# Sums of routed rows in a macaron mixture-of-experts kernel: the first choice weighed and added in one VectorE operation a tile, the second weighed on ScalarE

## The chip, the cores and the metric

One core of one Trainium2 chip runs the kernel. The time is device microseconds of one execution; three executions of the kernel before gave 1242.54, 1244.09 and 1245.39 us, so the median is 1244.09 us. The engines are TensorE (PE, its weight loads PEld), VectorE (DVE), ScalarE (ACT), GpSimd (POOL) and SyncE (SP, which issues most DMAs).

## The reference

The input is x of 8 batches of 1024 tokens of 256 channels, in float32. Three steps follow each other, all residual:

- x = x + 0.5 * FFN(layernorm(x))
- x = x + attention(layernorm(x)), a linear attention with relu on queries and keys, 16 heads
- x = x + 0.5 * FFN(layernorm(x)), the same weights

FFN is a mixture of 16 experts plus a shared expert. For each token a softmax gate chooses two experts (out of the two best of four groups), and the routed part is

```
y = w1 * expert_a(x) + w2 * expert_b(x)
```

with w1 and w2 the gate's scores of the first and the second choice. The change touches only this weighted sum and its adding to x.

## The kernel before, in words

All of x stays in SBUF as `xres`, 8 batches of 8 tiles; a tile is 128 tokens by 256 channels. An FFN first routes (scores, choices, ranks; rows of normalised tokens are scattered to DRAM in the order of experts), then runs 143 tiles of expert rows, whose outputs are scattered to a DRAM tensor `routed_rows` in the order (choice, token). The shared expert's work is cut into parts ("up" is two matmul groups with a silu on ScalarE and a gating on VectorE, "down" is a matmul group with two adds on VectorE), and these parts are spread over the stages: 19 of them are held back for the end of the second FFN (lines 248 and 257).

Both choices' rows come back from DRAM by DMA into a buffer `y` with the choice as an index of its own, and are weighed and added to `xres`. The weights, one for each token (a column of 128 x 1) and choice, already hold the factor 0.5. This happens at two places.

**After the first FFN, two tiles at a time** (a pair; 4 pairs a batch, 32 in all). SP loads a pair into one of three buffers once the pair three back is added (line 476). ScalarE's `weigh_routed` (line 1025) waits for the load and multiplies each of the four tiles (two tokens' tiles, two choices) by its weight in place. VectorE's `combine` (line 1474) waits for that, adds first choice, then second choice to x as two operations of 128 x 512, and takes the layer norm's statistics. The first batch's four pairs come ahead of the attention. The pairs of batch b+1 are placed inside the attention loop of batch b: on ScalarE behind every second relu of the keys (line 1107), on VectorE around `sum_keys` (lines 1593 to 1613). TensorE waits for `sum_keys` at line 764 and for the keys' relu at lines 732 and 743. In the batches b = 1, 3 and 5 of that loop the normalising and first routing of a batch of the second FFN is also done (line 898 on ScalarE); in b = 2, 4 and 6 the rest of its choice (VectorE). I call them the odd and the even batches.

**After the second FFN, four tiles at a time** (a piece; 2 a batch, 16 in all). SP loads six pieces ahead, and each later one when the piece six before it is added (lines 498 to 505), then stores the finished piece to the output. ScalarE runs, in order, the silu of one held part and then `weigh_final` of a piece (lines 1143 to 1146), eight multiplications. VectorE runs, in order, the held part's gating (line 1364) or two adds (line 1374), then the piece's two adds of 128 x 1024 (lines 1660 and 1662). Five held parts lie ahead of the first piece, one ahead of each of the next twelve pieces (up or down; two ups to a down), none ahead of the piece numbered 13, and a last down part ahead of piece 14. TensorE computes the held parts meanwhile.

The order on every engine is the order of the program; semaphores alone join them. The two places of waiting are, on VectorE,

```
dve.wait_ge(s.weighted, n + 1)          # pair: ScalarE has weighed both choices
dve.wait_ge(s.f_weighted, n + 1)        # piece
```

Of the kernel before, what the change touches and what calls it, by code (L numbers as in the profile page):

```python
# [18 lines left out]
ALU, ACT, AX = mybir.AluOpType, mybir.ActivationFunctionType, mybir.AxisListType  # L19

P = 128
BATCHES, SEQ, C = 8, 1024, 256
TOKENS = BATCHES * SEQ
NT = SEQ // P
# [25 lines left out]
YSLOTS = 3  # L50
# [4 lines left out]
PIECES = 2  # L55
FSLOTS = 6
# [198 lines left out]
def held_ahead(n):  # L255

    return HELD[1][n + 4 if n else 0:n + 5]
# [55 lines left out]
def program(nc, m, d, sem):  # L313
    s = Names()
# [64 lines left out]
    def x_tiles(b, i, n):  # L379
        return m.xres[:, b, i:i + n, :].rearrange("p i c -> p (i c)")  # L380

    def piece(n):
        b, h = divmod(n, PIECES)
        return x_tiles(b, h * NT // PIECES, NT // PIECES)
# [19 lines left out]
    with nc.Block() as block:  # L404
        @block.sync
        def _(sp):
# [5 lines left out]
            def pads(L):  # L412
                sp.wait_ge(s.pads_ready, L + 1)
                _, starts = nc.values_load_multi_w_load_instructions(
                    m.pad_to[0:1, :], engines=(sp.engine,), min_val=0, max_val=SPARE - P,
                    skip_runtime_bounds_check_because="a region holds a row for every token and a tile more")
                for start in starts:
                    sp.dma_start(d.xg[bass.ds(start, P), :], m.pad[:]).then_inc(s.padded, 16)
# [468 lines left out]
        def _(act):  # L887
# [128 lines left out]
                                             bias=m.tile_b13[:, 0, i:i + 1]).then_inc(s.rsilu_ready, 1)  # L1016

            def weigh(b, tiles, y):
                for k in range(2):
                    for j, i in enumerate(tiles):  # L1020
                        last = nc.scalar.activation(y[:, k, j * C:(j + 1) * C], y[:, k, j * C:(j + 1) * C], ACT.Copy,  # L1021
                                                    scale=m.weights[:, b, k, i:i + 1])
                return last

            def weigh_routed(b, h):
                n = PAIRS * b + h
                act.wait_ge(s.routed_in[n % YSLOTS], 16 * (n // YSLOTS + 1))
                weigh(b, range(2 * h, 2 * h + 2), m.ylq[:, n % YSLOTS]).then_inc(s.weighted, 1)

            def weigh_final(n):  # L1030
                b, h = divmod(n, PIECES)
                act.wait_ge(s.f_loaded[n % FSLOTS], 16 * (n // FSLOTS + 1))
                weigh(b, range(h * NT // PIECES, (h + 1) * NT // PIECES), m.yf[n % FSLOTS]).then_inc(s.f_weighted, 1)
# [44 lines left out]
            for i in range(PAIRS):  # L1078
                last = nc.scalar.activation(m.xs[0][:, i, 0:C], m.xres[:, 0, i, :], ACT.Identity,
                                            bias=m.nmr[:, i:i + 1], scale=m.rstd[:, i:i + 1])  # L1080
# [68 lines left out]
        def _(dve):  # L1149
            TT, TR = nc.vector.tensor_tensor, nc.vector.tensor_reduce  # L1150
            ch = Chain(dve, s.dve_steps)
# [7 lines left out]
            def stats(b, tiles, own=m.own):  # L1159
                for i in tiles:  # L1160
                    last = nc.vector.bn_stats(own.stat[:, i, :], m.xres[:, b, i, :])  # L1161
                ch.did(last)
# [213 lines left out]
            def shared(L, n, work, steps):  # L1376
                b, kind, k = part_of(n)
                r = L * BATCHES + b
                if b == BATCHES or kind == "up":
                    for _ in range(steps):  # L1380
                        next(work, None)
                    if b < BATCHES:
                        gated(r, k)
                    return
                for j in range(2):
                    add_shared(r, 2 * k + j)
                    for _ in range(steps * j // 2, steps * (j + 1) // 2):
                        next(work, None)
# [61 lines left out]
            def experts(L):  # L1450
                for i in range(-1, TILES + 2):
# [11 lines left out]
                    if routed(i - 2):  # L1463
# [7 lines left out]
                            dve.wait_ge(s.rows_out[last_user % SLOTS], 16 * (last_user // SLOTS) + 16)  # L1471
                        TT(m.ry[(i - 2) % RYSLOTS], ry_ps[y % RB][:, 0:C], m.be2[:, bass.ds(e, C)], ALU.add).then_inc(s.ry_scaled, 1)  # L1472

            def combine(b, h):
                n = PAIRS * b + h
                y = m.ylq[:, n % YSLOTS]
                dve.wait_ge(s.bias_added, BIASED.index(b) + 1)
                x = x_tiles(b, 2 * h, 2)
                dve.wait_ge(s.weighted, n + 1)
                ch.then(TT(x, x, y[:, 0, :], ALU.add))  # L1480
                TT(x, x, y[:, 1, :], ALU.add).then_inc(s.combined, 1)
                dve.wait_ge(s.combined, n + 1)
                stats(b, range(2 * h, 2 * h + 2))
# [169 lines left out]
            for n in range(BATCHES * PIECES):  # L1653
                b, h = divmod(n, PIECES)
                x, y = piece(n), m.yf[n % FSLOTS]
                for part in held_ahead(n):
                    shared(1, part, iter(()), 0)
                dve.wait_ge(s.bias_added, BATCHES + BIASED.index(b) + 1)
                dve.wait_ge(s.f_weighted, n + 1)
                TT(x, x, y[:, 0, :], ALU.add).then_inc(s.f_added, 1)  # L1660
                dve.wait_ge(s.f_added, 2 * n + 1)
                TT(x, x, y[:, 1, :], ALU.add).then_inc(s.f_added, 1)

# [224 lines left out]
```

## Time and profile before

| what | us |
|---|---|
| median of three runs | 1244.09 |
| the profiled execution, its own time | 1243.24 |
| its span, first to last instruction | 1241.5 |
| PE busy | 1148.4 (93%) |
| DVE busy | 852.7 (69%) |
| ACT busy | 759.6 (61%) |
| POOL busy | 698.1 (56%) |

The 1.7 us between the span and the execution's own time lie around the instructions. Shares of busy time are means over stages that have different limits. The two places of the change lie at 457 to 750 us (the pairs) and at 1180 to 1238 us (the pieces).

How to read the rows: a line of a timeline has the start in us, the duration in us (of all instructions merged into the line), the engine, the line of the kernel, the operation, output and inputs, and in brackets the idle time before it and what ended that. Consecutive instructions of one engine may overlap a little, so merged durations are less than the sum of single ones.

### The profile page before, as it was taken

What the parts mean: (1) busy time and instruction counts of PE and PEld (TensorE: products, weight loads), DVE (VectorE), ACT (ScalarE), POOL (GpSimd) and SP (SyncE); (2) the same over time, 40 slices, a digit from 0 to 9 for tenths busy, and PEclk for the clock granted to TensorE, in tenths of its full rate; (3) what the DMA queues carried; (4) which work ended last, traced back from release to release, by engine and by line L of the source; (5) the groups of instructions that cost most, each with busy time, mean ns of one, the idle gap of its engine ahead of it and who ended that gap; (6) DMA issues with size and microseconds to landing.
All of it is one profiled execution on the core that took longest, in us unless ns stands there. A gap on an engine that the chain in (4) does not pass through costs nothing.

```text
span 1241.5 us, 26349 instructions
## 1 busy us (share of the span) xinstructions
PE 1148.4 (93%) x6696; PEld 904.6 (73%) x6696; DVE 852.7 (69%) x2774; ACT 759.6 (61%) x1698; POOL 698.1 (56%) x850
## 2 busy tenths in 40 slices
PE   7988999999999967899998999889998999999995
PEld 5555555899999946777887878545557999999653
DVE  6788784566666655768878786677844666666488
ACT  4454441688888845675655653544415888888398
POOL 3577776488888854000411503356763888887810
PEclk9999999999999998999999999899999999999997
DMA  9922227556555523012320400114585555555398
GB/s 360 309 91 95 98 104 201 172 172 174 171 172 156 164 104 105 32 38 68 112 72 24 133 22 35 35 69 141 171 210 180 173 170 174 173 157 162 119 400 333
DMA packets 94215, 181.53 MB, mean 146 GB/s; under 512 B 17624, under 2 KB 60400, under 8 KB 92022
## 3 DMA queue, kind: packets, MB, share of 16 engines
q1 hardware_dynamic: 66630, 110.44, 29.2%
q0 software_dynamic: 26016, 67.55, 15.3%
q10 hardware_dynamic: 1424, 1.86, 0.5%
q8 instruction: 59, 0.97, 0.3%
q14 instruction: 86, 0.70, 0.2%
HBM read 97.63 MB, written 86.08 MB: 148 GB/s over the span
## 4 chain that ended last, share of the span: by engine, by line
PE 58%; DVE 17%; ACT 11%; issue 5%; POOL 5%; DMA 3%; SPq 1%; DVEq 0%; ACTq 0%; POOLq 0%
PE bank L700 20%; PE bank L710 10%; PE bank L559 7%; PE bank L691 5%; POOL expert_rows L1683 4%; PE bank L575 4%; PE bank L806 3%; ACT rows L1021 3%; ACT w L1021 3%; DVE stat L1161 2%; PE bank L756 2%; PE bank L732 2%; ACT xn L1039 1%; PE bank L521 1%; ACT rows L898 1%
## 5 line engine op out<-in xcount | busy, mean ns | idle before, releaser
L700 PE MATMUL bank<-rows,att 128*128 128x128 f32 x2288 | 303.2, 276 | 0.3 <-ACT att L1010 0.3
L700 PEld LDWEIGHTS bank<-rows,att 128*128 128x128 f32 x2288 | 279.2, 192 | 0.8 <-ACT att L1010 0.6
L1683 POOL DMA_INDIRECT expert_rows<-rows,slots x160 | 155.4, 971 | 80.0 <-issue 57.3
L1010 ACT COPY att<-w 128x512 f32 x286 | 177.0, 619 | 10.2 <-issue 4.2
L1740 POOL DMA_INDIRECT routed_rows<-silu,rdest x160 | 158.3, 989 | 35.0 <-issue 24.6
L1458 DVE SCALAR_TENSOR_TENSOR rows<-bank,tile_b,att 128x128 f32<-128x128 f32 x286 | 100.1, 350 | 112.9 <-ACT att L1015 102.0
L710 PE MATMUL bank<-w,rows 128*128 x572 | 171.5, 382 | 4.3 <-DVE rows L1458 4.2
L1740 POOL DMA_INDIRECT routed_rows<-rows,rdest x126 | 124.7, 990 | 68.4 <-DVE rdest L1441 40.7
L1009 ACT COPY rows<-bank 128x256 f32<-128x256 f32 x286 | 106.6, 373 | 89.1 <-PE bank L691 86.9
L575 PE MATMUL bank<-ws,be 128*128 128x256 f32 x512 | 124.0, 388 | 8.6 <-DVE be L1364 8.6
L925 ACT ACTIVATE silu<-bank,bs 128x512 f32<-128x512 f32 x64 | 43.9, 686 | 127.6 <-PE bank L559 117.5
L575 PEld LDWEIGHTS bank<-ws,be 128*128 128x128 f32 x512 | 95.8, 194 | 35.4 <-DVE be L1364 18.5
L1729 POOL TENSOR_TENSOR xres<-xres,half_bs 128x128 f32<-128x128 f32 x256 | 118.0, 470 | 3.1
L691 PE MATMUL bank<-ident,rows 128*128 128x128 f32 x572 | 109.4, 274 | 3.4 <-DMA rows<-expert_rows 2.0
L1015 ACT ACTIVATE att<-bank,tile_b 128x128 f32<-128x128 f32 x286 | 103.8, 363 | 4.5 <-PE bank L700 4.5
L691 PEld LDWEIGHTS bank<-ident,rows 128*128 128x128 f32 x572 | 80.4, 142 | 32.7 <-issue 3.8
L710 PEld LDWEIGHTS bank<-w,rows 128*128 128x128 f32 x572 | 87.2, 192 | 5.6 <-issue 5.5
L1683 POOL DMA_INDIRECT expert_rows<-w,slots x48 | 48.3, 1006 | 59.9 <-PE bank L732 28.0
L1364 DVE SCALAR_TENSOR_TENSOR be<-bank,bs,silu 128x512 f32<-128x512 f32 x64 | 47.7, 749 | 48.3 <-PE bank L559 43.6
L1680 POOL TENSOR_TENSOR rstd<-ve,minus_half 128x8 f32<-128x8 f32 x8 | 15.0, 1880 | 113.4 <-DVE ve L1169 113.4
L1472 DVE TENSOR_TENSOR silu<-bank,be 128x256 f32<-128x256 f32 x160 | 67.9, 424 | 15.2 <-issue 6.3
L1021 ACT ACTIVATE rows<-rows,weights 128x256 f32<-128x256 f32 x176 | 73.8, 504 | 7.3 <-DMA rows<-routed_rows 7.3
(212 smaller groups left out, 2156.9 us busy)
## 6 DMA issues: line engine op xcount, KB each, us to landing
rows<-expert_rows SPq DMA_DIRECT2D x286, 129.5 KB
rows<-routed_rows SPq DMA_DIRECT2D x32, 512.0 KB, 4.2
w<-routed_rows SPq DMA_DIRECT2D x10, 1024.0 KB, 10.9
out<-xres SPq DMA_DIRECT2D x16, 512.0 KB, 9.3
xres<-in_x SPq DMA_DIRECT2D x7, 1024.0 KB, 9.5
rows<-routed_rows SPq DMA_DIRECT2D x6, 1024.0 KB, 7.7
expert_rows<-pad SPq DMA_DIRECT2D x47, 129.5 KB, 14.0
w<-in_w SPq DMA_DIRECT2D x1, 4096.0 KB, 24.4
```

Of the source, the lines that this page charges most:

```text
L575: last = nc.tensor.matmul(y_ps[j][:, t % 2 * C:(t % 2 + 1) * C], m.gT[:, g, mi, t * P:(t + 1) * P], m.ws2[:, mi, :], start=mi == 0, stop=m ...
L691: last = nc.tensor.transpose(rT_ps[a % 2][:, c * P:(c + 1) * P], m.rin[:, a % SLOTS, c * P:(c + 1) * P], m.ident[:])
L700: last = nc.tensor.matmul(rh_ps[t % RB][:, n * P:(n + 1) * P], m.rw13[:, t % RB, c * C + n * INTER:c * C + (n + 1) * INTER], m.rT[:, t % R ...
L710: nc.tensor.matmul(ry_ps[y % RB][:, 0:C], m.rgT[:, y % RB, :], m.w2[:, bass.ds(e, C)], start=True, stop=True).then_inc(s.ry_ready, 1)
L1009: nc.scalar.copy(m.rT[:, a % RB, :], rT_ps[a % 2][:, 0:C]).then_inc(s.rT_copied, 1)
L1010: nc.scalar.copy(m.rw13[:, a % RB, :].rearrange("p (c n) -> p c n", c=KC), w13[:, :, bass.ds(expert_at(i + 2), C)]).then_inc(s.rw13_copied, 1)
L1015: nc.scalar.activation(m.rsilu[:, t % RB, :], rh_ps[t % RB][:, 0:P], ACT.Silu, bias=m.tile_b13[:, 0, i:i + 1]).then_inc(s.rsilu_ready, 1)
L1021: last = nc.scalar.activation(y[:, k, j * C:(j + 1) * C], y[:, k, j * C:(j + 1) * C], ACT.Copy, scale=m.weights[:, b, k, i:i + 1])
L1458: nc.vector.scalar_tensor_tensor(m.rgT[:, t % RB, :], rh_ps[t % RB][:, P:2 * P], m.tile_b13[:, 1, i:i + 1], m.rsilu[:, t % RB, :], ALU.add ...
L1683: nc.gpsimd.indirect_dma_start(out=d.xg, out_offset=bass.IndirectOffsetOnAxis(ap=m.slots[:, slots_of(r), k, i:i + 1], axis=0), in_=m.xs[bu ...
L1729: last = nc.gpsimd.tensor_tensor(x, x, m.half_bs2[:, c:c + P], ALU.add)
L1740: nc.gpsimd.indirect_dma_start(out=d.yt, out_offset=bass.IndirectOffsetOnAxis(ap=m.rdest[:, n:n + 1], axis=0), in_=m.ry[i % RYSLOTS], in_o ...
```

## The change

ScalarE weighs only the second choice. VectorE weighs and adds the first choice's rows with one `scalar_tensor_tensor` a tile: x = y * weight + x, the weight being a column of 128 x 1. These operations wait for the load and not for ScalarE; the second choice's add waits for ScalarE as before, and for the last of these operations.

```diff
             def weigh(b, tiles, y):
-                for k in range(2):
-                    for j, i in enumerate(tiles):
-                        last = nc.scalar.activation(y[:, k, j * C:(j + 1) * C], y[:, k, j * C:(j + 1) * C], ACT.Copy,
-                                                    scale=m.weights[:, b, k, i:i + 1])
+                for j, i in enumerate(tiles):
+                    last = nc.scalar.activation(y[:, 1, j * C:(j + 1) * C], y[:, 1, j * C:(j + 1) * C], ACT.Copy,
+                                                scale=m.weights[:, b, 1, i:i + 1])
                 return last
...
+            def weigh_and_add(b, tiles, y):
+                for j, i in enumerate(tiles):
+                    x = m.xres[:, b, i, :]
+                    last = nc.vector.scalar_tensor_tensor(x, y[:, 0, j * C:(j + 1) * C], m.weights[:, b, 0, i:i + 1], x,
+                                                          ALU.mult, ALU.add)
+                return last
+
             def combine(b, h):
                 n = PAIRS * b + h
                 y = m.ylq[:, n % YSLOTS]
                 dve.wait_ge(s.bias_added, BIASED.index(b) + 1)
                 x = x_tiles(b, 2 * h, 2)
+                dve.wait_ge(s.routed_in[n % YSLOTS], 16 * (n // YSLOTS + 1))
+                ch.did(weigh_and_add(b, range(2 * h, 2 * h + 2), y))
                 dve.wait_ge(s.weighted, n + 1)
-                ch.then(TT(x, x, y[:, 0, :], ALU.add))
+                ch.settle()
                 TT(x, x, y[:, 1, :], ALU.add).then_inc(s.combined, 1)
...
                 dve.wait_ge(s.bias_added, BATCHES + BIASED.index(b) + 1)
+                dve.wait_ge(s.f_loaded[n % FSLOTS], 16 * (n // FSLOTS + 1))
+                weigh_and_add(b, range(h * NT // PIECES, (h + 1) * NT // PIECES), y).then_inc(s.f_added, 1)
                 dve.wait_ge(s.f_weighted, n + 1)
-                TT(x, x, y[:, 0, :], ALU.add).then_inc(s.f_added, 1)
                 dve.wait_ge(s.f_added, 2 * n + 1)
                 TT(x, x, y[:, 1, :], ALU.add).then_inc(s.f_added, 1)
```

## Rows read from the trace of the kernel before

**Rows 1.** The page, part 4: the chain that ended last, by engine.

```profile
PE 58%; DVE 17%; ACT 11%; issue 5%; POOL 5%; DMA 3%; SPq 1%; DVEq 0%; ACTq 0%; POOLq 0%
```

**Rows 2.** Busy time by stretch: stretch, length, engines, PE clock, DMA share, GB/s.

```profile
1200.00:1210.00 10.00, 10.00 (x33) 5.96 (x32) 9.04 (x11) 10.00 (x25) 0.00 (x0) 1.00 1.03 401
```

**Rows 3.** The timeline of the pieces: start, duration, engine, line, idle before.

```profile
1181.16 0.75 DVE L1364 SCALAR_TENSOR_TENSOR be<-bank,bs,silu 128x512 f32<-128x512 f32 x1 [2.74 <-PE bank L559]
...
1211.05 1.28 DVE L1374 SCALAR_TENSOR_TENSOR xres<-bank,xres 128x512 f32<-128x512 f32 x2
...
1211.62 0.69 ACT L925 ACTIVATE silu<-bank,bs 128x512 f32<-128x512 f32 x1
...
1212.19 3.32 ACT L1021 ACTIVATE w<-w,weights 128x256 f32<-128x256 f32 x8
1212.25 1.21 DVE L1660 TENSOR_TENSOR xres<-xres,w 128x1024 f32<-128x1024 f32 x1
...
1213.50 1.22 DVE L1662 TENSOR_TENSOR xres<-xres,w 128x1024 f32<-128x1024 f32 x1
...
1214.64 0.74 DVE L1364 SCALAR_TENSOR_TENSOR be<-bank,bs,silu 128x512 f32<-128x512 f32 x1
...
1222.34 0.71 ACT L925 ACTIVATE silu<-bank,bs 128x512 f32<-128x512 f32 x1
...
1225.37 0.74 DVE L1364 SCALAR_TENSOR_TENSOR be<-bank,bs,silu 128x512 f32<-128x512 f32 x1
...
1226.17 6.36 PE L575 MATMUL bank<-ws,be 128*128 128x256 f32 x16 [3.58 <-DVE be L1364]
...
1231.94 1.33 DVE L1374 SCALAR_TENSOR_TENSOR xres<-bank,xres 128x512 f32<-128x512 f32 x2
...
1237.18 1.22 DVE L1662 TENSOR_TENSOR xres<-xres,w 128x1024 f32<-128x1024 f32 x1
```

**Rows 4.** VectorE's groups by form: line, operation, shape, count, busy us, mean ns.

```profile
L1458 DVE SCALAR_TENSOR_TENSOR rows<-bank,tile_b,att 128x128 f32<-128x128 f32 x286 | 100.1, 350 | 112.9 <-ACT att L1015 102.0 <-PE bank L710 9.8 <-issue 0.3
...
L1364 DVE SCALAR_TENSOR_TENSOR be<-bank,bs,silu 128x512 f32<-128x512 f32 x64 | 47.7, 749 | 48.3 <-PE bank L559 43.6 <-ACT silu L925 3.7
L1374 DVE SCALAR_TENSOR_TENSOR xres<-bank,xres 128x512 f32<-128x512 f32 x64 | 43.5, 688 | 41.0 <-PE bank L575 40.1 <-DVE weights L1310 0.4
```

**Rows 5.** The timeline at the experts' end, VectorE: two neighbours without a wait.

```profile
442.32 0.35 DVE L1458 SCALAR_TENSOR_TENSOR rows<-bank,tile_b,att 128x128 f32<-128x128 f32 x1 [0.29 <-ACT att L1015]
442.58 0.20 DVE L1441 TENSOR_SCALAR rdest<-rf,rows 128x1 uint32<-128x1 f32 x1
```

**Rows 6.** ScalarE's weighing, line 1021: durations in ns, minimum, median, maximum.

```profile
L1021 ACT ACTIVATE rows<-rows,weights x176: 492/498/543, 457.2 to 1228.9; 128x256 f32<-128x256 f32 x176
```

**Rows 7.** The timeline of the first batch's pairs, VectorE.

```profile
457.55 0.69 DVE L1374 SCALAR_TENSOR_TENSOR xres<-bank,xres 128x512 f32<-128x512 f32 x1 [0.96 <-PE bank L575]
459.05 0.69 DVE L1480 TENSOR_TENSOR xres<-xres,rows 128x512 f32<-128x512 f32 x1 [0.81 <-ACT rows L1021]
...
461.17 0.68 DVE L1480 TENSOR_TENSOR xres<-xres,rows 128x512 f32<-128x512 f32 x1
...
468.20 0.64 DVE L1167 BATCH_NORM_AGGREGATE mv<-stat 128x2 f32<-128x6 f32 x8
```

**Rows 8.** TensorE's waits, 632 to 671 us (an even batch): us, times, longest.

```profile
PE bank L764 <- DVE rows L1497: 1.6, 1, 1.6
```

**Rows 9.** TensorE's waits, 512 to 553 us (b = 1): us, times, longest.

```profile
PE bank L732 <- ACT be L1057: 1.9, 2, 1.0
PE bank L743 <- ACT be L1057: 0.7, 1, 0.7
```

**Rows 10.** The timeline of TensorE in b = 3, the last keys and queries.

```profile
610.07 2.22 PE L743 MATMUL bank<-be,xn 128*128 128x256 f32 x8
...
612.57 1.89 PE L756 MATMUL bank<-w_att,xnT 128*128 128x256 f32 x8
```

**Rows 11.** TensorE's waits, 476 to 512 us (b = 0): us, times, longest.

```profile
PE bank L764 <- DVE rows L1497: 0.3, 1, 0.3
```

## The prediction

> **What bounds the kernel now.** I read the page's chain first: over the whole span TensorE holds most of it, ScalarE and VectorE about a tenth and a sixth [rows 1], so a gain for ScalarE can count only in the stretches where it ends the waits. The busy time by stretch shows one: in the pieces at the end ScalarE is busy for all of 10 us, VectorE for 9.04, TensorE for 10, and the DMA engines' share is 1.03 [rows 2]. Four resources are full at once there. The timeline tells who sets the pace. Over a triple of pieces (two with an up part, one with a down part) ScalarE runs without a gap from 1211.62 to 1222.34, 10.72 us: two silus and 24 weighings, which start 0.40 apart ((3.32 - 0.50) / 7) [rows 3, 6]. VectorE waits for it at most pieces. ScalarE never waits for a load there, so the full DMA engines have not been the limit yet.
>
> In the attention loop TensorE is nearly always busy, and what counts is its few waits. In each of the even batches b = 2, 4 and 6 it waits 1.6 us for `sum_keys` [rows 8], one of three equal ones. In b = 1 it waits 1.9 and 0.7 us for the keys' relu, which stands behind the weighing on ScalarE [rows 9]. In b = 0 it waits 0.3 us for `sum_keys` [rows 11]. Ahead of the loop the first four pairs are a chain by themselves, since TensorE has nothing until they are normalised [rows 7].
>
> **The price of the new operation.** No row has a `scalar_tensor_tensor` of 128x256 with a column of weights, but two rows have one of other widths: 350 ns for 128 and 749 for 512 elements [rows 4]. The slope is 399 / 384 = 1.04 ns an element, so 256 take 0.35 + 0.133 = 0.483 us. The column costs about 0.06 of that: with an immediate in its place 512 elements take 688 [rows 4]. Neighbours without a dependence overlap by 0.09: two of 0.688 take 1.28 together [rows 3, 4], and behind an operation with a column the next starts 0.26 after it, which itself took 0.35 [rows 5]. So I take 0.39 from start to start, and a dependent operation 0.04 after the end, as 1212.25 + 1.21 to 1213.50 [rows 3]. The bounds: 0.33, if the column were read while the operation in front still runs, and 0.483, if nothing overlapped. I take 0.39, because [rows 5] is a neighbour of this very kind.
>
> The Trainium skill ("VectorE: DVE Perf Modes", The DRAIN you can't avoid) says that the next VectorE operation does not start until the one in front has emptied its pipe, and advises few operations. By that rule the interval is the upper bound; the rows just named disagree by 0.09 us. The same page (Two Vector instructions with no wait between them) has the hold only for operands that start in other quadrants, which these rows, all of full partitions, agree with.
>
> **A piece.** ScalarE loses four of eight weighings, 4 x 0.40 = 1.6 us. VectorE loses an add of 128x1024, which occupies it for 1.21 + 0.04 = 1.25, and gains 3 x 0.39 + 0.483 + 0.04 = 1.70 before the last add can start: 0.45 more. Its piece is then 1.70 and the last add, 1.14 to the next start (1213.50 to 1214.64 [rows 3]), 2.84. An up part adds 0.66 (0.749 less the overlap), a down part 1.20 (1.28 less the overlap). The triple is 2 x 3.50 + 4.04 = 11.04 us against ScalarE's 10.72 now. ScalarE needs only 10.72 - 12 x 0.40 = 5.9, so the **stall goes from ScalarE to VectorE, and VectorE is late next**.
>
> The way through the stage: the gating ahead of the first piece starts at 1181.16, because TensorE is done then [rows 3], and the new operations follow it at 1181.82 instead of waiting for ScalarE. The first piece ends (next start) at 1181.82 + 2.84 = 1184.66. Then eight up pieces, four down pieces and one without a part: 1184.66 + 8 x 3.50 + 4 x 4.04 + 2.84 = 1231.66. Before, these last two adds start at 1231.94. The head start is eaten up. They wait for TensorE's last part, which runs from 1226.17 for 6.36 us, behind the gating at 1225.37 [rows 3]; by the same sum that gating is at 1184.66 + 7 x 3.50 + 4 x 4.04 = 1225.3. So the second add ends its turn at about 1233.2, the piece's next start is 1236.0, and the last piece ends at 1236.0 + 2.84 + 0.09 = 1238.9, against 1237.18 + 1.22 = 1238.40. **Pieces: +0.5 us.** What is behind it, the last store, is as it was. The wait for the load costs nothing: ScalarE waited for the same load before, and loads are six pieces ahead; if a load came late, both engines would wait as one did.
>
> **The first four pairs.** The new operations can start when VectorE's last held add is over, 457.55 + 0.60 = 458.15, instead of 459.05 [rows 7]. A pair takes 2.12 now (459.05 to 461.17). It loses an add (0.69 + 0.04 to the next start) and gains 0.39 + 0.483 + 0.04 = 0.91: +0.18, so 2.30. The aggregate starts at 458.15 + 4 x 2.30 + 0.1 = 467.45 instead of 468.20 [rows 7]. **-0.7 us.**
>
> **Pairs in the loop.** Where VectorE's chain ends the wait, each pair costs 0.18: in b = 2, 4 and 6, four pairs each, 0.73 longer at `sum_keys` on top of the 1.6 [rows 8]: **+2.2 us**. In b = 1 two weighings lie between the first and the last of the three waits for the relu; they shorten it by 2 x 0.80. The first wait (1.0) stays and is 0.2 later, since the layer norm's factors come behind a pair on VectorE; of the other 1.6 [rows 9] about 0.3 stays. **-1.3 us.** In b = 0 the weighing is over earlier and VectorE, then idle, is done with both pairs in time: **-0.3 us** [rows 11], the wait itself being the most. In b = 3 and 5 one group of keys runs for 2.22 where the same shape takes 1.89 [rows 10], a wait for the last relu of some 0.3; ScalarE's 1.6 less removes most: **-0.25 us each**. The DMAs of the pairs are issued when a pair is added, so they move with it by tenths and stay three buffers ahead; nothing else is moved past a queue.
>
> **Sum:** +0.5 - 0.7 + 2.2 - 1.3 - 0.3 - 0.5 = -0.1 us. Against the profiled execution's own 1243.24 us that is 1243.1; that execution lies 0.85 under the median of 1244.09. On the median I forecast **1244.0 us, no change** (within 0.2%, 2.5 us, which is about what a measurement of this kernel tells from none).
>
> **Rivals.**
> *The column is read ahead* (interval 0.33, price 0.42 at the block's end). Then a piece costs 4 x 0.06 = 0.24 less, 3.8 us for 16, and a pair 0.12 less: 0.5 in the first four, 1.4 in the even batches. Together 5.7: 1238.3 on the median. For it speaks that only one kind of neighbour shows the interval, and its operand lies in PSUM; against it that this neighbour does pay it [rows 5]. Chance 0.2.
> *Slower: nothing overlaps.* Interval 0.483: a piece costs 3 x 0.09 = 0.27 more, 4.3 for 16, a pair 0.09 more, 0.4 in the first four, 1.1 in the even batches, 0.3 in b = 1. Together 6.1: 1250.1. It decides from where VectorE's triple passes ScalarE's 10.72, an interval of about 0.37, and is worse with each hundredth. Against it are the two overlaps above [rows 3 to 5]. By the skill's rule of the drained pipe this is the one to expect; the trace so far denies it. Chance 0.12.
> *The DMA engines take over.* With share 1.03 [rows 2] they may have no room for a faster piece. That caps a gain of the first rival at about half (1241); it changes nothing in my forecast, in which pieces get no faster. Chance 0.08.
>
> **How the numbers follow.** My own case has 0.6. Its terms are differences of waits, each sure to some tenths; the even batches and the pieces are repeated sums, in which 0.03 us an interval is 1.4 us for the pieces and 0.4 in the loop, so it spans 1241 to 1247, and leaves 0.05 of its chance beyond 2.5 us on the fast side and 0.08 on the slow one. Faster: 0.2 of the first rival, and 0.05 and some of the third: 0.26. Slower: 0.12 and 0.08: 0.2. Same: 0.54. The range reaches into the first rival and part of the second: 1239 to 1248.
>
> **What would show it.** In the profile after: the new operations at 0.48 us each and 0.39 apart; VectorE without idle time in the pieces and ScalarE idle there; a triple of 11.0 us from gating to gating; the wait at line 764 at 2.3 us in the even batches and none in b = 0; no waits for the relu over 0.3 us in b = 1 but the first; the aggregate at 467.5. Wrong would be: VectorE still waiting for ScalarE in the pieces, an interval under 0.36 (then it is faster), or one over 0.44 (then slower).

## The result, and the profile after

The changed kernel takes 1248.24 us (median of eleven executions, 1245.92 to 1251.48) where the kernel before takes 1244.13 in the same set of runs. A twelfth execution, a disturbed one of 3084 us, is left out here, while the expectations below count it into their 1248.38 and their +4.25. The ratio is 1.0035, 95% interval 1.0021 to 1.0048: **some 4 us slower** (4.1 by the medians, 4.4 by the ratio), between 2.6 and 6.0. A second set gave 1.0028 (1.0016 to 1.0040). The forecast was 1244.0 and no change. The profiled execution took 1247.44 us, its span is 1245.6.

**The pieces.** The timeline of VectorE over the same stage as [rows 3]; L1476 is the new operation, L1671 the second choice's add, L1363 the gating, L1373 the down part's adds:

```profile
1182.29 0.75 DVE L1363 SCALAR_TENSOR_TENSOR be<-bank,bs,silu 128x512 f32<-128x512 f32 x1 [2.74 <-PE bank L559]
1182.95 3.05 DVE L1476 SCALAR_TENSOR_TENSOR xres<-rows,weights,xres 128x256 f32<-128x256 f32 x4
1186.11 1.23 DVE L1671 TENSOR_TENSOR xres<-xres,rows 128x1024 f32<-128x1024 f32 x1
1187.25 0.75 DVE L1363 SCALAR_TENSOR_TENSOR be<-bank,bs,silu 128x512 f32<-128x512 f32 x1
1187.91 1.66 DVE L1476 SCALAR_TENSOR_TENSOR xres<-rows,weights,xres 128x256 f32<-128x256 f32 x4
1189.68 1.23 DVE L1671 TENSOR_TENSOR xres<-xres,rows 128x1024 f32<-128x1024 f32 x1
...
1194.93 0.74 DVE L1363 SCALAR_TENSOR_TENSOR be<-bank,bs,silu 128x512 f32<-128x512 f32 x1
...
1206.18 0.75 DVE L1363 SCALAR_TENSOR_TENSOR be<-bank,bs,silu 128x512 f32<-128x512 f32 x1
...
1241.36 1.23 DVE L1671 TENSOR_TENSOR xres<-xres,w 128x1024 f32<-128x1024 f32 x1
```

Four new operations take 1.66 us, and one takes 0.48 by VectorE's groups below: (1.66 - 0.48) / 3 = 0.39 from start to start. That is the price forecast. Three things are to be seen besides. The dependent add starts 0.11 after the end of the new ones (1187.91 + 1.66 = 1189.57, next start 1189.68), not 0.04. The first piece's four take 3.05. And behind the first gating VectorE waits for nothing but TensorE's last part (0.22 at 1236.07): a triple takes 11.25 us (1194.93 to 1206.18) where 11.04 was forecast, which is three times the missing 0.07. From the gating ahead of the first piece to the last add's end the stage takes 1242.59 - 1182.29 = 60.30 us; before it took 1238.40 - 1181.16 = 57.24 [rows 3]. A second profile of the changed kernel has 59.99; there VectorE does not wait for TensorE's last part. VectorE's groups by form:

```profile
L1363 DVE SCALAR_TENSOR_TENSOR be<-bank,bs,silu 128x512 f32<-128x512 f32 x64 | 47.8, 749 | 50.7 <-PE bank L559 45.9 <-ACT silu L925 3.6
...
L1476 DVE SCALAR_TENSOR_TENSOR xres<-w,weights,xres 128x256 f32<-128x256 f32 x40 | 16.6, 478 | 0.0
```

Where the rows lie in the other buffer the mean is 498, since that group holds the slow one of the first piece, the maximum of this row (durations in ns, minimum, median, maximum):

```profile
L1476 DVE SCALAR_TENSOR_TENSOR xres<-rows,weights,xres x88: 465/479/1865, 458.8 to 1233.4; 128x256 f32<-128x256 f32 x88
```

The busy time of ten us in the stage (stretch, length, busy time of PE, PEld, DVE, ACT and POOL, clock, DMA share, GB/s), against [rows 2]:

```profile
1200.00:1210.00 10.00, 9.34 (x29) 5.16 (x28) 9.69 (x18) 6.15 (x14) 0.00 (x0) 1.00 1.03 396
```

ScalarE fell from 10.00 to 6.15, VectorE rose from 9.04 to 9.69, and TensorE, full before, now has gaps. The load was moved past the point of balance.

**The attention loop.** TensorE's waits in an even batch (632 to 671 us) and in b = 1 (512 to 553), against [rows 8, 9]:

```profile
PE bank L764 <- DVE rows L1505: 2.7, 1, 2.7
...
PE bank L732 <- ACT be L1056: 1.2, 1, 1.2
```

In b = 1 the wait fell from 1.9 and 0.7 to 1.2. In the even batches it rose from 1.6 to 2.65. And something new stands behind it. TensorE in b = 4:

```profile
651.76 0.59 PE L756 MATMUL bank<-w_att,xnT 128*128 128x256 f32 x2
655.02 2.07 PE L764 MATMUL bank<-rows,ones_f 128*128 128x256 f32 x4 [2.66 <-DVE rows L1505]
...
663.71 1.03 PE L780 MATMUL bank<-w_att,att 128*128 128x256 f32 x4
```

TensorE in b = 4 of the kernel before:

```profile
654.20 1.13 PE L764 MATMUL bank<-rows,ones_f 128*128 128x256 f32 x4 [1.60 <-DVE rows L1497]
...
661.24 1.03 PE L780 MATMUL bank<-w_att,att 128*128 128x256 f32 x4
```

The matmuls at L764 (two in the program; the profile has two rows for each of these in float32) take 2.07 us where they take 1.13 elsewhere, and the way from L764 to L780 takes 8.69 us, against 7.04 before and in b = 2. The windows tell why; the first two are of the changed kernel in b = 4, the third is its b = 2, and the last two are of the kernel before in b = 4:

```profile
654.00:657.00 3.00, 1.98 (x5) 1.61 (x6) 0.93 (x2) 0.60 (x1) 1.92 (x1) 0.66 0.39 147
657.00:660.00 3.00, 3.00 (x15) 2.59 (x14) 2.23 (x5) 0.81 (x2) 0.00 (x0) 0.77 0.00 0
...
574.00:577.00 3.00, 2.23 (x10) 2.00 (x11) 1.24 (x3) 0.97 (x2) 1.75 (x1) 1.00 0.34 126
...
654.00:657.00 3.00, 2.80 (x13) 2.49 (x14) 1.24 (x3) 0.97 (x2) 1.22 (x1) 1.00 0.16 61
657.00:660.00 3.00, 3.00 (x20) 2.74 (x19) 2.79 (x9) 1.75 (x4) 0.00 (x0) 1.00 0.00 0
```

TensorE stood idle for 2.66 us, and then the granted clock is 0.66 and 0.77, a mean of stretches at the lower level (1.2 GHz) and at the full one (2.4 GHz). Before, it is 1.00 in both windows. The same happens in b = 6, and not in b = 2, although the wait is as long. What a fall costs is read from one start of L764 to the next, with and without it. The changed kernel's b = 2, 3, 4 and 5:

```profile
574.77 1.13 PE L764 MATMUL bank<-rows,ones_f 128*128 128x256 f32 x4 [2.65 <-DVE rows L1505]
...
614.46 1.07 PE L764 MATMUL bank<-rows,ones_f 128*128 128x256 f32 x4
...
655.02 2.07 PE L764 MATMUL bank<-rows,ones_f 128*128 128x256 f32 x4 [2.66 <-DVE rows L1505]
...
695.64 1.07 PE L764 MATMUL bank<-rows,ones_f 128*128 128x256 f32 x4
```

From b = 2 to b = 3 it is 39.69 us, from b = 4 to b = 5, behind a fall, 40.62: 0.93 more. From b = 6 to b = 7 it is 38.93 behind a fall, and 38.07 in the run with few bias adds (below), whose clock does not fall there: 0.86 more. The two falls cost 1.8 us in all.

I measure the loop from the start of L764 in b = 0 to its start in b = 7. This takes 278.19 us before and 281.28 after. Ahead of the loop the first four pairs, against [rows 7]:

```profile
458.24 0.69 DVE L1373 SCALAR_TENSOR_TENSOR xres<-bank,xres 128x512 f32<-128x512 f32 x1 [0.96 <-PE bank L575]
458.84 0.87 DVE L1476 SCALAR_TENSOR_TENSOR xres<-rows,weights,xres 128x256 f32<-128x256 f32 x2
459.82 0.69 DVE L1489 TENSOR_TENSOR xres<-xres,rows 128x512 f32<-128x512 f32 x1
...
461.22 0.86 DVE L1476 SCALAR_TENSOR_TENSOR xres<-rows,weights,xres 128x256 f32<-128x256 f32 x2
...
468.43 0.64 DVE L1166 BATCH_NORM_AGGREGATE mv<-stat 128x2 f32<-128x6 f32 x8
```

From the last held add to the aggregate it is 10.19 us now (468.43 - 458.24) and was 10.65: 0.46 gained. Loop and pieces together lose 3.1 + 3.1, less 0.46: 5.7 us in these traces, near the upper end of the interval that was measured.

### The profile page after: what moved, and what is told of

It reads as the page before. It is cut to its first block, busy times and chain, and to the rows that moved or that the text cites. A ratio compares the mean times of both kernels' runs of the same rounds, so it can differ in the third digit from the quotient of the medians.

```text
span 1245.6 us, 26349 instructions
## 1 busy us (share of the span) xinstructions
PE 1151.6 (92%) x6696; PEld 908.0 (73%) x6696; DVE 869.6 (70%) x2854; ACT 711.6 (57%) x1570; POOL 696.5 (56%) x850
## 4 chain that ended last, share of the span: by engine, by line
PE 61%; DVE 21%; issue 6%; POOL 4%; ACT 4%; DMA 2%; SPq 1%; DVEq 0%; ACTq 0%; POOLq 0%
PE bank L700 20%; PE bank L710 10%; PE bank L559 8%; PE bank L691 5%; PE bank L575 5%; POOL expert_rows L1692 4%; DVE xres L1476 3%; PE bank L806 3%; PE bank L756 3%; DVE stat L1160 3%; PE bank L732 2%; PE bank L743 2%; PE bank L521 1%; DVE xres L1489 1%; DVE xres L1373 1%
## 5 line engine op out<-in xcount | busy, mean ns | idle before, releaser
L1363 DVE SCALAR_TENSOR_TENSOR be<-bank,bs,silu 128x512 f32<-128x512 f32 x64 | 47.8, 749 | 50.7 <-PE bank L559 45.9
L1434 DVE TENSOR_TENSOR rf<-rows,rev_of 128x2 f32<-128x2 f32 x286 | 59.1, 207 | 29.0 <-DMA routed_rows<-rows,rdest 14.9
```

## The experiments

| kernel | loop, us | pieces, us | ratio to before, 95% |
|---|---|---|---|
| before, two profiles | 278.19, 278.21 | 57.24, 57.24 | 1 |
| changed, two profiles | 281.28, 281.25 | 60.30, 59.99 | 1.0035; 1.0028 |
| pieces only | 278.14 | 60.03 | 1.0030 (1.0016 to 1.0043) |
| pairs only | 281.08 | 57.23 | 1.0020 (1.0007 to 1.0032) |
| ScalarE's wait first | 279.88 | 58.89 | 1.0012 (0.9999 to 1.0026) |
| few bias adds | 280.26 | 58.58 | 1.0028 (1.0014 to 1.0043) |
| 16 filler matmuls | 281.66 | 59.99 | 1.0049 (1.0035 to 1.0062) |
| 8 filler matmuls | 279.77 | 60.07 | 1.0016 (1.0003 to 1.0028) |
| half of the pairs | 276.60 | 57.22 | 0.9986 (0.9974 to 0.9997) |
| half of the pairs, one tile of a piece | 276.58 | 54.83 | 0.9972 (0.9959 to 0.9984) |

Where a kernel leaves a stage as it was before, the stage repeats to 0.1 us for the loop and to 0.02 for the pieces, so tenths are read from the two middle columns. The pieces as changed spread by 0.3 (59.99 to 60.30). The ratios carry about 1.5 us either way (0.0012 x 1247), and tell only the sign and the rough size; those of the sixteen fillers and of the last row come from five and six executions, the others from eleven or twelve.

**Pieces alone.** `combine` and the pairs' weighing as before, the pieces changed. The edit is against the changed kernel; the last argument of `weigh` lists the choices that ScalarE weighs.

```diff
-                weigh(b, range(2 * h, 2 * h + 2), m.ylq[:, n % YSLOTS]).then_inc(s.weighted, 1)
+                weigh(b, range(2 * h, 2 * h + 2), m.ylq[:, n % YSLOTS], (0, 1)).then_inc(s.weighted, 1)
...
-                weigh(b, range(h * NT // PIECES, (h + 1) * NT // PIECES), m.yf[n % FSLOTS]).then_inc(s.f_weighted, 1)
+                weigh(b, range(h * NT // PIECES, (h + 1) * NT // PIECES), m.yf[n % FSLOTS], (1,)).then_inc(s.f_weighted, 1)
...
-                dve.wait_ge(s.routed_in[n % YSLOTS], 16 * (n // YSLOTS + 1))
-                ch.did(weigh_and_add(b, range(2 * h, 2 * h + 2), y))
                 dve.wait_ge(s.weighted, n + 1)
-                ch.settle()
+                ch.then(TT(x, x, y[:, 0, :], ALU.add))
```

> The pieces as changed, the pairs as before. My theory (the pieces cost by themselves: the first four new operations run against GpSimd's bias adds, 3.05 us instead of 1.66, and every last add starts 0.11 instead of 0.04 us behind them): 2.5 to 3.5 us over the kernel before, about 1247. Rival (the loss is made in the attention loop, the stage of the pieces only ends later because it begins later): within 1 us of before. In the trace, from the gating ahead of the first piece to the end of the last add: 60.3 us by my theory (58.5 or less is the way before, 57.2 + 1.2), the triple of pieces 11.25.

The pieces take 60.03 us, the loop is as before, with waits of 1.60 at L764 and no fall of the clock. Ratio 1.0030, 3.7 us: the pieces alone make the kernel slower.

**Pairs alone.** The other half.

```diff
-                weigh(b, range(2 * h, 2 * h + 2), m.ylq[:, n % YSLOTS]).then_inc(s.weighted, 1)
+                weigh(b, range(2 * h, 2 * h + 2), m.ylq[:, n % YSLOTS], (1,)).then_inc(s.weighted, 1)
...
-                weigh(b, range(h * NT // PIECES, (h + 1) * NT // PIECES), m.yf[n % FSLOTS]).then_inc(s.f_weighted, 1)
+                weigh(b, range(h * NT // PIECES, (h + 1) * NT // PIECES), m.yf[n % FSLOTS], (0, 1)).then_inc(s.f_weighted, 1)
...
-                dve.wait_ge(s.f_loaded[n % FSLOTS], 16 * (n // FSLOTS + 1))
-                weigh_and_add(b, range(h * NT // PIECES, (h + 1) * NT // PIECES), y).then_inc(s.f_added, 1)
                 dve.wait_ge(s.f_weighted, n + 1)
+                TT(x, x, y[:, 0, :], ALU.add).then_inc(s.f_added, 1)
```

> The pairs as changed, the pieces as before. My theory: the loop ends 3 us later than before (waits of 2.6 us at line 764 in b = 2, 4 and 6, and TensorE at a low clock behind some of them), of which the experts of the second FFN take back about two thirds, since they start by waiting for a load: 1 us over before. Rival (the loss is the loop's and stays): 3.5 to 4.5 us over before.

The loop takes 281.08 us, with a wait of 2.65 in each even batch and the slower way behind it in b = 4 and b = 6 (8.73 and 8.72 us). The pieces take 57.23. Ratio 1.0020, 2.4 us, which lies between the two forecasts of 1 and of 3.5 to 4.5. Each half loses by itself, and the two add up to what the whole change loses within the intervals (3.7 + 2.4 = 6.1 us, each with about 1.6 either way, where the whole change has 2.6 to 6.0).

**ScalarE's wait first.** The gap of 0.11 stands where VectorE passes two waits in a row ahead of the dependent add: one for ScalarE, one for its own last operation. Here the one for ScalarE is put ahead of the new operations, in both places.

```diff
                 dve.wait_ge(s.f_loaded[n % FSLOTS], 16 * (n // FSLOTS + 1))
+                dve.wait_ge(s.f_weighted, n + 1)
                 weigh_and_add(b, range(h * NT // PIECES, (h + 1) * NT // PIECES), y).then_inc(s.f_added, 1)
-                dve.wait_ge(s.f_weighted, n + 1)
                 dve.wait_ge(s.f_added, 2 * n + 1)
```

> As changed, but VectorE waits for ScalarE ahead of the new operations, so that between them and the last add only the wait for themselves is left. Theory A (two waits in a row make the gap of 0.11): the gap is 0.04 again, the pair takes 2.31 and the triple 11.04 us, the wait at line 764 is 2.35 us and TensorE's clock may stay at its upper level there: 1.5 to 3.5 us less than the changed kernel, 1245 to 1247. Theory B (the gap belongs to the new operation's own end): the gap stays 0.11 and the time within 1 us of the changed kernel, 1248.4.

VectorE's timeline of the second piece in this kernel:

```profile
1192.67 1.66 DVE L1476 SCALAR_TENSOR_TENSOR xres<-rows,weights,xres 128x256 f32<-128x256 f32 x4
1194.36 1.22 DVE L1671 TENSOR_TENSOR xres<-xres,rows 128x1024 f32<-128x1024 f32 x1
```

1192.67 + 1.66 = 1194.33, so the add starts 0.03 later. The pieces take 58.89 us, 1.1 to 1.4 less than in the changed kernel's two profiles (16 x 0.07 = 1.1), and the wait in the even batches falls from 2.65 to 2.38 (4 x 0.07 = 0.28). The second wait in a row costs 0.07 us though ScalarE had long been done. The four operations of the first piece still take 3.07, so the wait is not their cause. The clock fell again, this time in b = 2 and b = 6.

**Few bias adds.** While the first piece's new operations ran for 3.05 us, GpSimd was adding the shared expert's bias to other tiles of x. The changed kernel's GpSimd:

```profile
1170.89 13.23 POOL L1738 TENSOR_TENSOR xres<-xres,half_bs 128x128 f32<-128x128 f32 x32
```

These merged rows leave off at 1184.12, and one more of 0.47 follows, to 1184.53. Only the first of VectorE's four is slow, 1.865 us; it ends at 1184.82, 0.3 behind GpSimd's last add. The experiment leaves out 30 of the last 32; half of the shared bias is then missing in two batches of the output.

```diff
             for j in range(2 * (TILES // 3) + min(TILES % 3, 2), 2 * NT * BATCHES):
-                add_bias(1, j)
+                if j % (2 * NT) == 2 * NT - 1:
+                    add_bias(1, j)
```

> As changed, but GpSimd leaves out 30 of its last 32 bias adds (128x128 each) of the second FFN, so that half of the shared bias is missing in the outputs of two batches; nothing else waits for these adds. Theory A (the first piece's new operations are slow because GpSimd adds at the same time): they take 1.66 instead of 3.05 us, the stage ends 1.4 us earlier: 1247.0. Theory B (they are slow because the DMA engines are saturated with the first loads): still about 3.05 us, no change, 1248.4.

VectorE's timeline of the first piece in this kernel:

```profile
1186.80 0.75 DVE L1363 SCALAR_TENSOR_TENSOR be<-bank,bs,silu 128x512 f32<-128x512 f32 x1 [2.74 <-PE bank L559]
1187.46 1.66 DVE L1476 SCALAR_TENSOR_TENSOR xres<-rows,weights,xres 128x256 f32<-128x256 f32 x4
1189.23 1.23 DVE L1671 TENSOR_TENSOR xres<-xres,rows 128x1024 f32<-128x1024 f32 x1
```

1.66 again, and the stage takes 58.58 us, 1.7 and 1.4 less than in the two profiles of the changed kernel. GpSimd's adds are what made the first piece slow. The Trainium skill ("SBUF — State Buffer", Who interferes with whom) says that a VectorE instruction with two inputs in SBUF gets in the way of a GpSimd instruction that reads SBUF, and that one of the two then waits; the trace agrees, with four operations at 3.05 us beside GpSimd and 1.66 without it. The time as a whole did not show this gain (1.0028, in the same interval as the changed kernel's): 1.5 us is what a ratio can just not tell. The loop takes 280.26, since the clock fell once and not twice.

**Filler matmuls.** If it is TensorE's idle time that lets the clock fall, work without use in that time must keep it up. First sixteen matmuls were put there, then eight, since sixteen outlast the wait.

```diff
             def spread_ksum(b):
-                pe.wait_ge(s.ksum_ready, 2 * b + 2)
                 pe.wait_ge(s.g_copied, 2 * b + 2)
+                if b in (2, 4, 6):
+                    for _ in range(8):
+                        nc.tensor.matmul(ctx_ps[:, 0:P], m.ones_f[:], m.ident[:], start=True, stop=True)
+                pe.wait_ge(s.ksum_ready, 2 * b + 2)
```

> The changed kernel, with sixteen 128-column fp32 matmuls of no use put into TensorE's queue in batches 2, 4 and 6, ahead of its wait at L764 (their result is overwritten), so that TensorE works in most of the time in which it otherwise waits for VectorE. Theory A (the granted clock falls because TensorE stands idle there for longer than before): the clock stays 1.00 after the wait in all three batches, L764 to L780 takes 7.04 us each time in place of 8.7 in b=4 and b=6, b=0 to b=7 at L764 takes about 280 us in place of 281.28, and the kernel takes 1 to 2 us less than the changed one (+2.5 to +3.2 over before in place of +4.25). Theory B (the clock falls there for another reason, such as the whole load of the stretch before): L764 to L780 still takes 8.7 us in some of these batches and the time stays at +4.25.

With sixteen, no wait is left at `sum_keys` in the even batches, the clock does not fall, and the way to the mixer takes 6.94 us in all three. But the loop takes 281.66 us and the ratio is 1.0049: the fillers themselves hold TensorE for longer than it waited, 3.73 us for 2.65. That the fall goes with TensorE's idle time is borne out by this, the price is not.

> As the run with sixteen filler matmuls, but with eight: by that run's rows sixteen took some 4.3 us and so outlasted the wait of 2.65 us, eight take about 2.1 us and fit into it. Their result is overwritten, as there. Theory A (TensorE's idle time ahead of L764 is what lets the clock fall, the wait itself is VectorE's doing): a wait of about 0.5 us is left at L764's place in b=2, 4, 6, the clock stays 1.00, the way from it to L780's place takes about 7.0 us each time, b=0 to b=7 takes 279.4 to 280 us in place of 281.28, and the kernel takes about 1.5 us less than the changed kernel of the same call. Theory B (TensorE's queue cannot take these matmuls for nothing): b=0 to b=7 takes 281 us or more.

With eight, b = 4 on TensorE (again two rows for each matmul; the filler is L764 in this kernel, the keys' sum L767, the mixer's place L783), and the same two windows as above:

```profile
653.48 1.95 PE L764 MATMUL bank<-ident,ones_f 128*128 128x128 f32 x16
656.30 1.13 PE L767 MATMUL bank<-rows,ones_f 128*128 128x256 f32 x4 [0.87 <-DVE rows L1508]
...
663.34 1.03 PE L783 MATMUL bank<-w_att,att 128*128 128x256 f32 x4
```

```profile
654.00:657.00 3.00, 2.13 (x16) 1.88 (x16) 2.14 (x12) 0.60 (x1) 1.60 (x1) 1.00 0.61 188
657.00:660.00 3.00, 3.00 (x19) 2.74 (x19) 1.91 (x4) 0.97 (x2) 0.32 (x1) 1.00 0.03 8
```

The granted clock is 1.00, the way takes 7.04 us in all three batches, and the loop takes 279.77 us, 1.5 less than in the changed kernel. The wait that is left is 0.87 and not the 0.5 expected. In the same set of runs the changed kernel has 1.0028 and this one 1.0016; the intervals overlap, the direction is the trace's. So the **falls of the clock behind the longer wait cost 1.5 us net** by this run, and 1.8 by the starts of L764 in the changed kernel itself (above). Idle time is needed for it, but it does not decide alone: over all profiles the clock fell behind 9 of 15 waits of 2.37 to 2.66 us, behind none of the 15 of 1.6 us, and behind none of the 6 with fillers. What picks the batch was not found.

**Before and after once more.** The first two profiles suggested that the experts, which start later after the change, take part of the loss back.

> The kernel before once more, for a second profile of it. Theory A (the late start of routing in the changed kernel is partly taken back where the experts start, because there the kernel before waits for the be2 load): again TensorE waits some 3 us for VectorE at the experts' start, and from b=7 at L764 to the last gating ahead of the pieces it again takes some 392 us against 389.7 in the changed one. Theory B (this stretch varies by 2 to 3 us from run to run): another length, as 393 to 394.5 in three of the experiments. Under both the granted clock is 1.00 after the waits at L764 in all batches, and b=0 to b=7 takes 278.2 us.

> The changed kernel once more, on the same chip as the other and for a second profile. Theory A (loop and pieces cost the same each time, and the stretch of routing and experts varies by itself): b=0 to b=7 at L764 takes 281.3 us, the stage of the pieces 60.3 us, both within 0.5, and the stretch between them anything from 390 to 394.5; the time is 1.0035 of before within 0.0015. Theory B (the later start of routing is taken back by the experts, as the first profile suggested): again about 389.7 us for the stretch between.

The loop came out the same in both, the pieces too but for 0.3 after the change (table). From L764 in b = 7 to the gating ahead of the first piece it took 409.42 and 411.17 us before, 407.16 and 408.97 after (the two texts give this stretch as some 17.4 us shorter); over all the kernels here it ran from 407.2 to 412.0. It took 410.2 on the mean of the five profiles whose loop is under 279 us, and 408.8 on that of the four whose loop is over 281, so there may be a give-back of some 1.5 us, but in each of the two groups the profiles lie 2 us or more apart. At the experts' start TensorE waits 3.40 us for VectorE in the first profile of before; in the second it waits 3.61 us for a load of rows instead. The stretch varies by more than what was to be explained in it, so the give-back can neither be shown nor excluded, and the difference between 5.7 us by the stages and 3.5 to 4.4 by the runs stays open.

**Half of the pairs, then also one tile of a piece.** If the new operation pays where ScalarE is late and costs where VectorE is, the split should follow that. The pairs of batches 0, 2, 4 and 6 are summed the new way; they stand ahead of the loop and in b = 1, 3 and 5. In the second kernel VectorE also takes one of a piece's four first-choice tiles. The edit of the second, against the kernel before, cut to its main lines; the first has 0 for the last argument of the pieces' `weigh` and no change in the pieces on VectorE:

```diff
-            def weigh(b, tiles, y):
+            def weigh(b, tiles, y, added):
                 for k in range(2):
                     for j, i in enumerate(tiles):
-                        last = nc.scalar.activation(y[:, k, j * C:(j + 1) * C], y[:, k, j * C:(j + 1) * C], ACT.Copy,
-                                                    scale=m.weights[:, b, k, i:i + 1])
+                        if k or j >= added:
+                            last = nc.scalar.activation(y[:, k, j * C:(j + 1) * C], y[:, k, j * C:(j + 1) * C], ACT.Copy,
+                                                        scale=m.weights[:, b, k, i:i + 1])
...
-                weigh(b, range(2 * h, 2 * h + 2), m.ylq[:, n % YSLOTS]).then_inc(s.weighted, 1)
+                weigh(b, range(2 * h, 2 * h + 2), m.ylq[:, n % YSLOTS], 0 if b % 2 else 2).then_inc(s.weighted, 1)
...
-                weigh(b, range(h * NT // PIECES, (h + 1) * NT // PIECES), m.yf[n % FSLOTS]).then_inc(s.f_weighted, 1)
+                weigh(b, range(h * NT // PIECES, (h + 1) * NT // PIECES), m.yf[n % FSLOTS], 1).then_inc(s.f_weighted, 1)
...
+                dve.wait_ge(s.f_loaded[n % FSLOTS], 16 * (n // FSLOTS + 1))
                 dve.wait_ge(s.f_weighted, n + 1)
-                TT(x, x, y[:, 0, :], ALU.add).then_inc(s.f_added, 1)
+                first = h * NT // PIECES
+                weigh_and_add(b, range(first, first + 1), y)
+                TT(x[:, 1 * C:], x[:, 1 * C:], y[:, 0, 1 * C:], ALU.add).then_inc(s.f_added, 1)
```

> Pairs of batches 0, 2, 4, 6 summed by the new way (these are the first four pairs and those that stand in loop turns 1, 3 and 5), those of batches 1, 3, 5, 7 and all pieces as before. Theory A (the change pays where ScalarE is late and costs where VectorE is the late one): loop turns 1, 3, 5 give back 1.4, 0.3 and 0.3 us, turns 2, 4, 6 wait 1.6 us at L764 as before without a fall of the clock, b=0 to b=7 takes about 276.2 us in place of 278.2, the first four pairs give some 0.4 more, the stage of the pieces takes 57.2, and the kernel is 1 to 2.4 us faster than before (ratio 0.998 to 0.9992). Theory B (what the loop gains is lost again in the routing and the experts, which are set by scatters and loads): b=0 to b=7 is as short, but the time is as before within 0.5 us.

The loop takes 276.60 us, 1.6 less than before (2.0 expected), with waits of 1.61 and 1.62 at L764 and no fall of the clock. The ratio is 0.9986, 1.8 us faster. What the loop gained was not all lost later (the interval is 0.4 to 3.2 us).

> As the run with the pairs of batches 0, 2, 4, 6 alone, and in the pieces VectorE weighs and adds one of the four tiles of the first choice, ScalarE the other three and all four of the second. Theory A (before, ScalarE's eight weighings of some 0.43 us set the pace of a piece, about 3.58 us, and TensorE's parts follow just under it): the stage of the pieces takes 55 to 56.5 us in place of 57.24, and the kernel is 1 to 2 us faster than with the pairs alone, 2 to 4 us faster than before. Theory B (VectorE is the bound in the pieces already with the extra 0.1 us that one new operation adds): 57.5 to 58.5 us and no gain over the pairs alone.

The pieces take 54.83 us, 2.4 less than before, a little better than expected. VectorE's timeline of one triple in this kernel, and the busy time of the same ten us as above:

```profile
1193.75 0.75 DVE L1365 SCALAR_TENSOR_TENSOR be<-bank,bs,silu 128x512 f32<-128x512 f32 x1
1194.41 0.48 DVE L1478 SCALAR_TENSOR_TENSOR xres<-w,weights,xres 128x256 f32<-128x256 f32 x1
1194.80 0.95 DVE L1677 TENSOR_TENSOR xres<-xres,w 128x768 f32<-128x768 f32 x1
1195.79 1.23 DVE L1679 TENSOR_TENSOR xres<-xres,w 128x1024 f32<-128x1024 f32 x1
...
1204.07 0.74 DVE L1365 SCALAR_TENSOR_TENSOR be<-bank,bs,silu 128x512 f32<-128x512 f32 x1
```

```profile
1200.00:1210.00 10.00, 10.00 (x33) 5.96 (x32) 9.76 (x14) 9.38 (x24) 0.00 (x0) 1.00 1.03 397
```

A triple takes 10.32 us (1193.75 to 1204.07) against 10.72 before [rows 3] and 11.25 after the change. In these ten us neither ScalarE nor VectorE is full, and TensorE is, and ScalarE's silu waits for TensorE once a triple (0.62 us at 1201.10): the held parts set the pace here. The DMA engines' share is 1.03 as before, and still the stage became 2.4 us shorter, so they did not cap it, as the prediction's third rival would have had it. The ratio is 0.9972 (0.9959 to 0.9984), **3.5 us faster than before**, and the stages add up to 1.6 + 2.4 = 4.0.

## Why the prediction was wrong

By its steps:

- **The price of the operation: right.** Forecast 0.483 us and 0.39 apart, measured 0.48 and 0.39. Both rivals about the interval fall: neither a column read ahead (0.33) nor operations that don't overlap (0.483). By the rule of the drained pipe in the Trainium skill ("VectorE: DVE Perf Modes", The DRAIN you can't avoid) four would take 4 x 0.48 = 1.92 us, and they take 1.66; but the same section says that a next operation that is not held starts earlier, which the prediction left out there, and with that the trace agrees.
- **The stall goes to VectorE: right.** It waits for ScalarE nowhere in the pieces, and ScalarE has 3.85 us of ten to spare.
- **"A dependent operation 0.04 after the end": wrong.** It is 0.11 where the wait for ScalarE stands between. I took 0.04 from a pair of adds with a single wait between them [rows 3]. The change itself adds the second wait, and the prediction counted waits only by whom they wait for. The error is 0.07 x 16 = 1.1 us in the pieces and 0.28 in each even batch. Shown by the run with ScalarE's wait first.
- **"The new operations follow it at 1181.82 instead of waiting for ScalarE": the start is right, their duration there wrong.** Behind the first gating they ran beside GpSimd's bias adds and took 1.4 us more. Before, the wait for ScalarE kept VectorE's first add back until 1183.42, and there GpSimd was done but for 0.05 us, by its timeline in the kernel before at 1169.81 + 13.66 = 1183.47:

```profile
1169.81 13.66 POOL L1729 TENSOR_TENSOR xres<-xres,half_bs 128x128 f32<-128x128 f32 x33
...
1183.42 1.23 DVE L1660 TENSOR_TENSOR xres<-xres,rows 128x1024 f32<-128x1024 f32 x1 [1.51 <-ACT rows L1021]
```

  The wait that was removed had hidden the collision. I read the rows of three engines there, and not those of the fourth. With these two the forecast of +0.5 becomes 0.5 + 1.1 + 1.4 = 3.0; measured 3.06, and 2.75 in the second profile. The head start that the sum gave to the first piece was spent on GpSimd.
- **Even batches, "+2.2": too small twice.** The wait grew by 1.04 in each and not by 0.73, nearly all of it the 0.28 of the second wait: 3.1 us, and the batches in front of these waits are 0.2 longer besides. And the longer wait let TensorE's clock fall, 1.8 us net, which no term held. A wait was priced as time, not as what TensorE does after it.
- **b = 1, "-1.3": right in size**, 1.4. By its own words the sum there is 1.1, for the 0.2 by which the first wait grows was named and not taken off; that wait grew as said, from 1.0 to 1.2, and the 0.3 that was to stay of the others went. **b = 3 and 5, "-0.25 each": right** where it can be read: from L764 in b = 2 to its start in b = 3 it is 39.69 us, before 40.01. Behind b = 4 the clock's fall lies over it; in the run with ScalarE's wait first, where it did not fall there, it is 39.67 for 40.00.
- **b = 0, "-0.3": wrong, small.** The wait at L764 is 0.39, not gone. VectorE's second add there runs for 2.77 us while GpSimd still adds biases, to 482.25; before, its first add there ran for 1.52 us, and GpSimd was done at 481.65. By the rows it is the same collision as in the first piece, but no run tried it alone. Before and after:

```profile
480.68 1.52 DVE L1480 TENSOR_TENSOR xres<-xres,rows 128x512 f32<-128x512 f32 x1 [8.91 <-ACT rows L1021]
...
480.03 2.77 DVE L1489 TENSOR_TENSOR xres<-xres,rows 128x512 f32<-128x512 f32 x1 [6.78 <-ACT rows L1020]
```

- **The first four pairs, "-0.7": right in kind.** 0.46; four gaps of 0.07 are the rest.

Put together: 3.06 - 0.46 + 3.3 + 1.8 - 1.4 - 0.6 + 0.1 = 5.8 us, which is what the stages show (5.7, and 0.1 ahead of b = 0), against some 4 (2.6 to 6.0) measured; the rest is open, as said above. The balance was forecast to tip by nothing because gains and losses of a few tenths cancelled; three prices were missing, that of the second wait (1.1 + 3 x 0.28), of the collision (1.4) and of the clock (1.8), and all three had the same sign.

## What to carry to other kernels

Where two engines share work, move as much as evens them out and no more: a fused operation on the other engine pays in the stretches where the first engine is the late one, and the two kinds of stretch can be told apart by who ends TensorE's wait. Before work is started earlier, look at what every engine does in the time it moves into, the ones that take no part in the change too; a wait may be hiding a collision. And put a wait that is surely met ahead of the work rather than between two dependent operations.

## What the hardware showed that was not expected

- Two waits in a row ahead of a dependent VectorE operation: it starts 0.11 us after the end of the one in front; with one wait 0.03 to 0.04.
- A VectorE operation with two inputs from SBUF, weighing one with a column: 0.48 us by itself, up to 1.865 beside GpSimd's adds of 128 x 128.
- TensorE's granted clock fell behind 9 of 15 waits of 2.37 to 2.66 us in the middle of the loop, where TensorE is otherwise nearly always busy, and cost about 1.65 us on the way that follows (8.7 for 7.04). Part of that comes back in a later wait: L806's in b = 4 is 0.6 us where 1.2 stood, so that a fall costs about 0.9 in the end.
